# Merged FFN and recurrence program: scan steps kept out of two runs of matrix products in each round, smaller work quotas, and the attention front stage moved to other places

## What is computed

```python
x = x + 0.5 * _L0_ffn_ref(_layernorm(x, axis=-1), ...)   # causal MoE block, 8 experts, top 2
x = x + _L0_attn_ref(_layernorm(x, axis=-1), ...)        # 5-level block attention
x = x + 0.5 * _L0_ffn_ref(_layernorm(x, axis=-1), ...)   # the MoE block again
x = x + 0.5 * _L1_ffn_ref(_layernorm(x, axis=-1), ...)   # binarised MLP, 128-512-128
x = x + _L1_attn_ref(_layernorm(x, axis=-1), ...)        # recurrence over 1024 steps, then an MLP
x = x + 0.5 * _L1_ffn_ref(_layernorm(x, axis=-1), ...)   # the binarised MLP again
```

```python
def step(state, inp):
    xb_t, xd_t = inp
    state = jnp.tanh(state @ A.T + xb_t)
    out = state @ C.T + xd_t
    return (state, out)
...
y = _layernorm(out_seq + x, ln_w, ln_b)
h = jax.nn.gelu(jnp.einsum('bth,fh->btf', y, W1) + b1, approximate=False)
y = y + jnp.einsum('btf,hf->bth', h, W2) + b2
```

## Time and profile before

| | |
|---|---|
| median of 3 runs | 2390.83 us (2367.38 to 2404.4) |
| the profiled execution | 2389.97 us, its span 2388.2 us |
| TensorE matmul busy | 2025.7 us (85%) |
| TensorE weight load busy | 1427.6 us (60%) |
| VectorE busy | 1007.5 us (42%) |
| ScalarE busy | 842.0 us (35%) |
| GpSimd busy | 191.7 us (8%) |
| mean granted clock | 0.691 |

### The profile page before, as it was taken

The page is one execution under the profiler, slowest core; times in us unless marked ns, Lnnn a source line. Parts: engine busy times, 40 slices in busy tenths (PEclk is TensorE's granted clock), DMA queues, the critical chain, the costliest instruction groups (busy, mean ns, idle before and its releaser), DMA issues.

```text
span 2388.2 us, 36502 instructions
## 1 busy us (share of the span) xinstructions
PE 2025.7 (85%) x13496; PEld 1427.6 (60%) x13496; DVE 1007.5 (42%) x3005; ACT 842.0 (35%) x2344; POOL 191.7 (8%) x314
## 2 busy tenths in 40 slices
PE   2898996678586885478989999999999999999986
PEld 1666764465474755365656666666666666666554
DVE  3667655766767786552123223231232222111201
ACT  1444435546465565132222322322223222222222
POOL 1221201010000100120000000000000000000000
PEclk8999996789697897685555766855556555555556
DMA  5000000000000000000000000000000000000000
GB/s 145 1 1 1 0 1 1 2 2 2 2 2 2 2 2 1 1 1 1 1 0 1 1 5 1 5 0 1 5 1 1 5 1 1 5 1 1 5 5 5
DMA packets 12015, 13.07 MB, mean 5 GB/s; under 512 B 1648, under 2 KB 10640, under 8 KB 11280
## 3 DMA queue, kind: packets, MB, share of 16 engines
q1 hardware_dynamic: 11840, 10.77, 1.7%
HBM read 8.67 MB, written 2.10 MB: 5 GB/s over the span
## 4 chain that ended last, share of the span: by engine, by line
issue 54%; POOL 3%; POOLq 1%; PE 0%; DVE 0%; ACT 0%; DVEq 0%; ACTq 0%
POOL r_pairs L716 1%; POOLq L685 1%; POOL r_roots L708 0%; POOL r_root_a L725 0%; POOL r_root_r L725 0%; POOLq L724 0%; POOL r_root_p L725 0%; POOL r_root_z L725 0%; PE r_up L852 0%; PE r_down L904 0%; POOLq L699 0%; POOLq L707 0%; POOLq L697 0%; POOLq L695 0%; POOLq L692 0%
## 5 line engine op out<-in xcount | busy, mean ns | idle before, releaser
L1047 ACT ACTIVATE r_state<-r_scan 32x4 f32<-32x4 f32 x1024 | 170.3, 166 | 917.7 <-PE r_scan L766 916.9
L766 PEld LDWEIGHTS r_scan<-r_state,rnnA 128*32 128x32 f32 x2048 | 181.1, 137 | 404.4 <-issue 322.8
L766 PE MATMUL r_scan<-r_state,rnnA 128*32 128x4 f32 x2048 | 270.0, 202 | 33.1 <-ACT r_state L1047 33.1
L877 PE MATMUL r_down<-moe,r_hT 128*128 128x128 f32 x1024 | 283.5, 423 | 0.0
L1311 DVE SCALAR_TENSOR_TENSOR x_all<-r_down,r_weight,x_all 128x128 f32<-128x128 f32 x256 | 72.1, 344 | 492.8 <-PE r_down L877 492.8
L852 PE MATMUL r_up<-r_x2T,moe 128*128 128x256 f32 x512 | 274.2, 645 | 4.2 <-ACT r_hT L1119 4.2
L877 PEld LDWEIGHTS r_down<-moe,r_hT 128*128 128x128 f32 x1024 | 213.2, 290 | 5.3
L2086 DVE TENSOR_TENSOR att_big<-at_ring,att_big 128x512 f16<-128x512 f32 x192 | 123.9, 684 | 49.4 <-ACT att_big L1768 48.6
L286 PEld LDWEIGHTS f_down<-moe,f_hT 128*128 128x128 f32 x1024 | 125.5, 194 | 27.8 <-issue 26.6
L1768 ACT ACTIVATE att_big<-at_ring 128x512 f16<-128x512 f32 x192 | 111.3, 596 | 66.7 <-PE at_ring L1901 64.8
L852 PEld LDWEIGHTS r_up<-r_x2T,moe 128*128 128x128 f32 x512 | 123.5, 293 | 13.5 <-ACT r_hT L1119 5.2
(11 more groups left out here) (306 smaller groups left out, 3338.7 us busy)
## 6 DMA issues: line engine op xcount, KB each, us to landing
x_all<-in_x SPq DMA_DIRECT2D x4, 512.0 KB, 6.1
moe<-in_moe SPq DMA_DIRECT2D x2, 1024.0 KB, 6.4
out<-x_all SPq DMA_DIRECT2D x8, 256.0 KB, 2.3
bin<-in_bin SPq DMA_DIRECT2D x2, 256.0 KB, 7.6
mlp<-in_mlp SPq DMA_DIRECT2D x2, 256.0 KB, 6.0
att_big<-in_att_wq SPq DMA_DIRECT2D x1, 512.0 KB, 10.0
att_big<-in_att_wk SPq DMA_DIRECT2D x1, 512.0 KB, 11.9
att_big<-in_att_wv SPq DMA_DIRECT2D x1, 512.0 KB, 13.9
```

Of the source, the lines that this page charges most:

```text
L766: nc.tensor.matmul(at(scan[b][0:STATE, :], t), rnnA[:, :], last, start=False, stop=(t == 127), skip_group_check=True).then_inc(s_step, 1)
L877: ins = nc.tensor.matmul(down[e % 2][:, s * 128:(s + 1) * 128], hT[c % H_RING][:, s * 128:(s + 1) * 128], w2[:, c * 128:(c + 1) * 128], st ...
L1047: nc.scalar.activation(at(state[b][0:STATE, :]), at(scan[b][0:STATE, :]), ACT.Tanh).then_inc(s_tanh, 1)
```

## The change

`spend` does nothing while the flag `dense` is set, so products run without steps between them. Two stretches are set so in each round: at its head the first two up products with `p_turn1` and `p_mix` between them, and in `second` the up products of "r" with the last expert's down products in their middle. `p_mix` moves from the round's start into the first of these runs and writes the bank `turn` instead of `front`. `QUOTA` falls (520 to 430 in rounds 1 to 4). The query products start at expert 1 instead of 3, `p_turn1` moves from expert 2 to the head, the router's place is expert 5 instead of 6. `qkv` gets a second buffer. On VectorE `v_stats` and `v_norm1` run in the round before, on GpSimd `a1` with them; "r" has three down chunks before the turn of "a" instead of two.

```diff
-        qkv = sb("qkv", [128, NB, QKV])
+        qkv = [sb(f"qkv{i}", [128, NB, QKV]) for i in range(2)]
...
-        TURN = {"a": down[0], "p": down[0], "r": front, "z": down[1]}
+        TURN = {"a": down[0], "p": down[0], "r": turn, "z": down[1]}
...
+                a1(2)
                 for g in range(-1, GROUPS + 1):
...
-                    if G + 2 < GROUPS:
-                        a1(G + 2)
...
                         rsqrt("z", h)
+                    if G + 3 < GROUPS:
+                        a1(G + 3)
...
                 def spend(ns):
 
+                    if dense[0]:
+                        return
...
                 def p_mix(g):
                     pe.wait_ge(s_tanh, ONE + 128 * (g + 1))
-                    pe.wait_ge(s_qkv, ONE + NB * fronts(g + 1))
+                    pe.wait_ge(s_gshift, ONE + min(g + 3, GROUPS))
...
+                    dense[0] = True
                     e_up(g, 0)
-                    for e in range(EXPERTS):
-                        if e + 1 < EXPERTS:
-                            e_up(g, e + 1)
-                        if ahead and e in (4, 5):
-                            p_qkv(g + 2, 2 * e - 7)
+                    if ahead:
+                        p_turn1(g + 2)
+                    if h >= 0:
+                        p_mix(h)
+                    e_up(g, 1)
+                    dense[0] = False
+                    e_down(g, 0)
+                    for e in range(1, EXPERTS - 1):
+                        e_up(g, e + 1)
+                        if e <= 3 and ahead:
+                            p_qkv(g + 2, e - 1)
+                        if e == 5 and back:
+                            p_turn3(g + 1)
                         e_down(g, e)
...
+                        if e == 3 and ahead:
+                            p_qkv(g + 2, 3)
...
-                        if e == 6 and back:
                             p_router(g + 1)
...
+                    dense[0] = True
                     if post:
-                        p_up("r", h)
-                        p_down("r", h, (0, 1))
+                        p_up("r", h, (0, 1))
+                    if pre:
+                        e_down(G, EXPERTS - 1)
+                    if post:
+                        p_up("r", h, (2, 3))
+                        dense[0] = False
+                        p_down("r", h, (0, 1, 2))
...
                 v_weights(0)
+                v_stats(2)
+                v_norm1(2)
                 for g in range(-1, GROUPS + 1):
...
-QUOTA = {-1: 0.0, 0: 450.0, 1: 520.0, 2: 520.0, 3: 520.0, 4: 520.0, 5: 480.0, 6: 480.0, 7: 300.0, 8: 0.0}
+QUOTA = {-1: 0.0, 0: 400.0, 1: 430.0, 2: 430.0, 3: 430.0, 4: 430.0, 5: 405.0, 6: 380.0, 7: 160.0, 8: 0.0}
```

More of the change, by code:

```diff
@@ L887, in p_turn, with p_up @@
                     turn_tiles(xn[k][g % 2], s_turn[k], TURN[k], ("turn", k, g))
-                def p_up(k, g):
+                def p_up(k, g, chunks=range(FC)):
                     pe.wait_ge(s_nT[k], ONE + g + 1)
-                    for c in range(FC):
+                    for c in chunks:
                         up_product(k, g, c, W1[k][:, c * 128:(c + 1) * 128], nT[k][g % 2])
@@ L1030, in _ @@
                         pause(3)
-                    second(g, G, h)
+                    second(G, h)
+                    if DBG: print('BODY', g, 'spent', spent[0], 'left', limit[0] - scanned[0])
+                    spent[0] = 0.0
                     pause(128)
@@ L1411, in experts @@
                             n_norm("r", h, mixed)
-                        if e == 1 and ahead:
-                            v_norm1(g + 2)
                         if e == 1 and back:
@@ L1423, in experts @@
                             v_norm2(g + 1)
-                            residual(g + 1)
-                        if e == 6 and ahead:
+                        if e == 4 and ahead:
                             v_scores(g + 2)
                             v_shift(g + 2)
-                        if e == 6 and back:
+                        if e == 5 and back:
                             v_logits(g + 1)
+                            residual(g + 1)
                 def second(G, h):
```

73 lines of the change are left out of this document (37 added, 36 removed).

## The result

The changed kernel takes 2017.62 us (median of 4 runs, 2013.95 to 2020.05); the kernel before, beside it, 2389.93 us (2367.38 to 2404.4). The ratio is 0.847, 95% interval 0.841 to 0.853. The forecast was 2100 with a range of 2020 to 2240: the direction and the mechanism came as told, and the time lies 2.4 us under the low end.

What follows compares the result with a forecast made beforehand. TensorE's list, run almost wholly at 1.2 GHz, was taken as the bound. 2388.2 - 247 (rounds 1 to 5) - 61 (round 6) - 30 (round 0) + 6 + 12 + 30 = 2098, plus 1.8 around the span: 2100 us, range 2020 to 2240.

Steps and rivals of the forecast that it cites:

- the units: TensorE price list: a down product 0.45 us at the low clock, 0.22 high; a step 0.45 and 0.36.
- first stretch: From the first expert's down products to the router in a round: 45 us if the high clock level holds.
- rest: Part of a round after the middle: 34.8 us at the high level plus seven more steps, together 37.3 us.
- Rival 1: Only the middle run lifts the clock; head and first part of each round stay low: 2300 us, chance 0.10.
- Rival 3: The clock level falls at the first turn of each long part of a round: about 2340 us, chance 0.04.
- Rival 4: ScalarE's table loads still cut both runs of products, so no run lifts the clock: 2475 us, chance 0.04.
- Rival 5: No net change: the runs lift the clock in one or two rounds alone; near 2390 us, chance 0.04.
- the rise inside the head: Sign expected in the profile after: TensorE's clock rises inside the head of each of rounds 1 to 6.
- falls on the way: Allowance for two of twelve long high-clock stretches dropping half-way, at about 15 us each: 30 us.
- waits in the rounds: Allowance for waits from moves costed at nothing, should their cover be gone: 2 us per round, 12 in all.
- round -1, with its start: Group 2's transposes wait for its normalisation on VectorE, 7.3 us and more, partly offset by a shorter wait: +6 us.
- Rival 2: The runs lift the clock sooner and the router does not end the high level: about 2027 us, chance 0.06.

## Why the prediction came out as it did

**Right.** The bound, the mechanism and the units, but for that of the mix: the gain is the clock; the runs lift it in the head and in the middle; it falls behind the router in rounds 1 to 4. Measured in rounds 3 and 4: bare steps 4.9 us (predicted 4.9), head 8.8 to 9.0 (8.8), first stretch 45.6 (45), router 1.1 (1.1), to the middle 10.1 to 10.4 (11.3, with nine steps where ten stand), middle 6.3 to 6.5 (8.3), rest 35.8 (37.3). Five rounds are 565.7 us instead of 584, round 6 103.1 instead of 105. Rivals 1, 3, 4 and 5 are out: both runs lift, no stretch falls at its turns, no wait of microseconds is left in rounds 1 to 6. One sign came in part: the rise inside the head is there in rounds 1, 3, 4 and 6, but in 2 and 5 it came only at the run's end.

**Mis-sized.** The sum was 2098 for the span, and it is 2018.3. The 80 us are, term by term:

| term | predicted | measured | difference |
|---|---|---|---|
| falls on the way | +30 | none | -30 |
| waits in the rounds | +12 | none of note | -12 |
| rounds 1 to 5 | 584 | 565.7 | -18 |
| round 0 | 118.8 | 105.0 | -14 |
| round 7 and tail | 146.7 | 141.1 | -6 |
| round 6 | 105 | 103.1 | -2 |
| round -1, with its start | +6 | +3.3 and +4.0 | +1 |

*Falls and waits* are the step that failed most: allowances without a row behind them, which make half of the miss. For the falls the rows even spoke against it, since the high stretch of the earlier trace rows had lasted to its end. No stretch to the router or to the round's end dropped half-way in the profiled execution.

*Rounds 1 to 5*: the middle run lifted the level after 3 us, the early rise of the earlier trace rows, not the late one that I took. In the rest, TensorE is busy for all of 35.80 us, while the earlier trace rows has 1.2 us of idle time that I carried along; the seven added steps took their place. That the head of rounds 3 and 4 came out at 8.8 is luck, since two errors cancel in it: its level rose after 3.0 to 3.4 us instead of 6, but a product of the mix costs 0.40 us at the high level, not the 0.22 of the unit (eight products from 1447.29 to 1450.52). The mix should have been priced from its own rows. The heads of rounds 2 and 5, where the level rose only at their end, took 13.3 and 12.8 us.

*Round 0*: I took the stretch of round 3 (84.8 less 49.3), less 5. Its own stretch is 45.5 us against 87.4 before, 41.9 less, since the 16 units that now stand behind the router are missing from it here as in the other rounds, and the sum for round 0 had left that out; the run at its head saves another 4.7 (6.1 us instead of 10.8); and the part behind the router, with those units and denser steps, is 3.7 longer (51.1 instead of 47.4).

*Round -1*: the wait is 9.57 us, in the 7 to 10 foreseen. The 4.0 us by which the loop started later do not look like the change's: kernels with the same prologue started at 1018 to 1025 us.

Rival 2 had the rise right in part, and the router wrong in four of five rounds; its 2027 is near the time by luck, because it left out the allowance for falls.

**Where the expectations on the runs failed.** The kernel without runs gained 5%, where I had it even with before: I had not foreseen that the level rises in rounds 2 to 5 where no run stands, and why it is high for longer there than in the kernel before is not shown. I took the last expert's products in the middle to be needed against the table loads; without them the wait is 1.4 us and the level rises all the same. And in the old order I took the router's run to save 18 us and the moves to be worth nothing; it saved 3, since the level fell at other places, and the moves cover waits.

## What to carry to other kernels

Where one engine is busy all the time, look at its clock before its instruction count, and price each stretch at both levels from rows of the same trace: here the kernel runs in 0.85 of its time with no product less, because a latency chain was moved out of two short runs of products. In this kernel a lifted level often fell at the same few places, the router, the bare end of a round and the mix. What helped was to issue the router without steps (17 us), to leave fewer bare steps (16 us), and to keep a second run behind the place where the level falls most. Then look at the waits again: once the clock is won, they are what is left between two orders. When the terms of a sum are read from rows, don't add allowances that no row supports: they were half of the miss.

## What was not expected of the hardware

A run of 44 float32 transposes, 6.7 us of them, lifted TensorE's clock to its upper level as products do. And the upper level was often lost without TensorE being idle for more than some tenths of a microsecond: behind the eight-column products of the router and in the mix, whose products alternate between 32 and 128 rows (the two instructions of one take 0.48 us at the upper level and 0.79 at the lower), more often behind bare steps than behind full-sized up products. That the small shapes are the cause is not shown. The same list of instructions kept the level in some rounds and lost it in others.
